# Keys made earlier in the step, list rows a step later, and a step's indirect DMAs in one row behind its scores

## The chip, the cores and the metric

The kernel runs on one core of a Trainium2 chip. Its five engines run side by side and meet on semaphores: TensorE (PE) multiplies matrices into the PSUM banks, VectorE (DVE) and ScalarE (ACT) work elementwise, GpSimd (POOL) does small arithmetic and issues the indirect DMAs, and SyncE (SP) issues the plain ones. The metric is the time of one execution on the device in microseconds (us), as a median of several runs.

## The reference

Input x is 128 sequences of 64 tokens with 128 features (8192 tokens), the context is as large, the mask is all ones. Two gated layers follow each other:

```
x = x + tanh(g_xattn[0]) * attention0(layernorm(x), ctx, ctx)     # q,k,v with biases; 16 heads of 8, softmax / sqrt(8)
x = x + tanh(g_ffn[0])   * experts0(layernorm(x))                 # 8 experts, top 2 by the router, gelu, 128->512->128
x = x + tanh(g_xattn[1]) * attention1(ctx, ctx, layernorm(x))     # per-head 8x8 weights, softmax / sqrt(128)
x = x + tanh(g_ffn[1])   * experts1(layernorm(x))                 # 4 experts, relu, gated by a depth per token
```

All of it is computed in float32; only the router's choice and the softmax's shift are split into parts of lower precision so that the sums stay exact.

## The kernel before, in words

**Steps.** The tokens of a layer's attention are cut into 32 groups of 256 tokens (two tiles of 128; `GROUPS`). Each engine runs a function `step(g)` once per group, written out in a fixed order; group g's scores stand in step g and what follows from them in the next steps: the values are multiplied by the probabilities in step g+1, heads and output projection come in step g+2, the second layer norm and the router in step g+3. A call `now(work, d)` does a piece of work for group g+d.

**A step of layer 0 on TensorE** turns the first quarter of the last group's probabilities (`probs_turned`, L1656), multiplies this group's keys and queries (`scores`, L1613: 32 small matmuls, keys stationary), turns the heads of group g-2 (L1588), turns the tokens of g+1 (L1632), projects the heads of g-2 (`project_out`, L1639), turns the rest of the probabilities, subtracts the maxima for two of the four score banks (`less_maximum`, L1623), and then multiplies probabilities by values for g-1 (`values_by_probs`, L1671, 32 small matmuls) and makes keys and queries of g+1 (`keys_queries`, L1687 and L1692) into the first bank of `ps_s`.

**On ScalarE** the step copies out what TensorE turned (PT, OT, xnT, xn2T), takes the exponentials (L813) and at its end copies the queries (qT, L777) and the keys in block-diagonal form (Kbd, L823, four operations). The next step's scores need those. `kept` is the copy of the summed values.

**VectorE** takes maxima (L1080), subtracts them, does the residual, the layer norms and, in every fourth step, the router's choice for a block of four groups; `route_places` (L1181 on) turns that choice into places in the lists.

**The lists.** Each token's row goes to the lists of its two experts in DRAM by an indirect DMA of 128 rows (`scatter`, L632), two per tile, 128 in all. `rows_due(k)` says which rows are issued in step k: the four of group k-8 from step 8 on, and near the end what the table `LAST_ROWS` says, up to six in a step. `scatter_at` spreads them over POOL's step at the points A to F, between waits for DVE's maxima, for the values product and for `xc`. When all of layer 0 is through, the rest of the rows follows, SyncE fills the lists' unused ends with zeros and loads the experts' tiles. In layer 1 the rows come back by indirect loads (`gather`, L675), four per step, likewise spread over the step.

**Banks.** `jobs` and `bank_free` say who used a bank of PSUM last and what TensorE must wait for before it writes the bank again.

Of the kernel before, what the change touches and what calls it, by code (L numbers as in the profile page):

```python
# [74 lines left out]
def at(u, k, mult=1, add=0, per=2):  # L75

    if isinstance(u, int):
# [11 lines left out]
LAST_ROWS = {24: ((16, 0, 1), (17, 0)), 25: ((17, 1), (18, 0, 1)), 26: ((19, 0, 1), (20, 0)), 27: ((20, 1), (21, 0, 1)),  # L89
             28: ((22, 0, 1), (23, 0)), 29: ((23, 1),), 30: ((24, 0, 1), (25, 0)), 31: ((25, 1),),  # L90
# [77 lines left out]
def build(nc, A, out):  # L168
    with ExitStack() as ctx:
# [169 lines left out]
        def late_to(n, batch, head):  # L339
# [15 lines left out]
        kq_bank, lg_bank, rk_bank = (ps_s[:, i, :] for i in range(3))  # L355
# [51 lines left out]
            "XT": (xnT_ready, 1, 1),  # L407
            "XT2": (xn2T_ready, 1, 1), "V": (v_ready, 1, 1)}

        def jobs(bank, g):  # L410

            if bank == 6:
                found = [("OT", g.plus(-2)), ("OUT", g.plus(-2))]
            else:
# [175 lines left out]
        def _(pool):  # L590
# [44 lines left out]
            def rows_due(k):  # L635

                due = LAST_ROWS.get(k, ((k - 8, 0, 1),) if 8 <= k < GROUPS else ())
                return [(n, slot, t) for n, *slots in due for slot in slots for t in range(2)]

            def scatter_at(g, point):  # L640

                rows = rows_due(g.k)
                spots = {2: "AD", 4: "ABCD", 6: "ABCDEF"}.get(len(rows), "")
                if point in spots:
                    scatter(*rows[spots.index(point)])
# [33 lines left out]
            def step(g):  # L679
# [13 lines left out]
                if have(0):  # L693
                    pool.wait_ge(max_done, g.count(4, 1))
                if g.layer == 0:
                    scatter_at(g, "A")
                elif have(4):
                    gather(g.plus(4), 0, 0)
                if g.layer == 1 and g.k in (GROUPS - 2, GROUPS - 1):
                    split_chunk(0, g.k - (GROUPS - 2))  # L700
                if have(0):
                    pool.wait_ge(max_done, g.count(4, 3))
                if g.layer == 0:
                    scatter_at(g, "B")
# [3 lines left out]
                elif have(4):  # L708
                    gather(g.plus(4), 0, 1)
# [1286 lines left out]
```

## Time and profile before

| | before |
|---|---|
| median of 3 runs | 1203.03 us (1202.12 to 1204.2) |
| the profiled execution's own time | 1202.05 us |
| its span in the trace | 1200.3 us |
| mean clock granted to TensorE, as a share of full speed | 0.963 |
| busy: PE / DVE / ACT / POOL | 1083.8 / 894.5 / 794.5 / 543.2 us |
| layer 0, first scores to last scores | 14.00 to 345.79 us |
| rest of layer 0, end of the lists | 345.79 to 404.44 us |
| layer 1, first scores to last scores | 678.46 to 966.06 us |

The profiled execution is one run, within the spread of the runs. Between 404 and 678 us stand the expert tiles of layer 0, after 970 us the dense experts of layer 1; the change doesn't touch either. A step is the time from the first matmul of one group's scores to that of the next. A duration in a row is that of the instruction or of a run of like instructions that abut; what stands in brackets is the idle time of the engine just before and what ended it, which is inferred from semaphore events ("remote" or "issue" stand where no instruction of this core is found to have ended just then).

### The profile page before, as it was taken

The page shows a single profiled execution, that of the slowest core. Times are in us where ns is not written, and L with a number is a line of the kernel's source. Part 1 is how long each engine was busy: PE and PEld are TensorE (multiplying, and loading weights), DVE is VectorE, ACT ScalarE, POOL GpSimd, SP SyncE. Part 2 cuts the span into 40 slices and gives each one's busy share as a digit, 9 for nine tenths or more (in the row PEclk, how much of TensorE's full clock was granted, in tenths as well). Part 3 has the DMA queues.
Part 4 walks back from the last instruction along what each step waited for, and adds up shares of the span by engine and source line. Part 5 has one row for each costly group of instructions (what it writes and reads, how often), then busy time and mean ns, then how long its engine had stood idle before and what let it go on. Part 6 is the DMA issues. An engine that isn't in the chain of part 4 may idle for free.

```text
span 1200.3 us, 38909 instructions
## 1 busy us (share of the span) xinstructions
PE 1083.8 (90%) x13205; PEld 918.0 (76%) x13205; DVE 894.5 (75%) x3003; ACT 794.5 (66%) x1739; POOL 543.2 (45%) x699
## 2 busy tenths in 40 slices
PE   7799999997885499999999699999999988999998
PEld 4677777775763499999999567666666767999997
DVE  5678887886777445545545779899898878988886
ACT  4788888886671255555555489999998964444443
POOL 2114555556547344344343676676666431222230
PEclk7999999999897699999999899999999999999999
DMA  7223211111101233333332211111221100000000
GB/s 195 86 86 94 78 55 54 53 51 56 49 22 55 82 98 102 96 93 96 93 95 77 57 50 49 50 48 47 51 50 46 32 2 10 27 17 17 26 17 27
DMA packets 116776, 71.81 MB, mean 60 GB/s; under 512 B 51736, under 2 KB 105240, under 8 KB 116632
## 3 DMA queue, kind: packets, MB, share of 16 engines
q1 hardware_dynamic: 108440, 53.13, 16.2%
q0 software_dynamic: 8192, 16.79, 4.5%
q8 instruction: 87, 1.43, 0.5%
q14 instruction: 57, 0.47, 0.1%
HBM read 45.88 MB, written 22.94 MB: 57 GB/s over the span
## 4 chain that ended last, share of the span: by engine, by line
PE 69%; DVE 10%; ACT 7%; issue 7%; SPq 4%; another core or an unknown queue 1%; POOL 1%; DMA 1%; DVEq 0%; ACTq 0%; POOLq 0%
PE ps_m L1902 11%; PE ps_p L1656 6%; PE ps_p L1781 5%; PE ps_m L1781 4%; PE ps_s L1613 4%; PE ps_p L1671 4%; PE ps_s L1888 3%; PE ps_s L1889 3%; PE ps_s L1890 3%; PE ps_s L1623 3%; PE ps_m L1639 3%; PE ps_s L1769 2%; PE ps_s L1771 2%; PE ps_s L1770 2%; PE ps_m L1588 2%
## 5 line engine op out<-in xcount | busy, mean ns | idle before, releaser
L776 ACT ACTIVATE PT<-ps_p 128x512 f32<-128x512 f32 x320 | 184.4, 596 | 32.3 <-PE ps_p L1656 18.2
L1080 DVE TENSOR_REDUCE mx<-ps_s 128x8 f32<-128x512 f32 x256 | 169.3, 683 | 36.8 <-PE ps_s L1613 23.4
L877 ACT ACTIVATE Kbd<-ps_s,c 128x512 f32<-128x512 f32 x128 | 87.4, 687 | 113.9 <-PE ps_s L1771 113.6
L592 POOL TENSOR_TENSOR spare<-spare 1x1 f32<-1x1 f32 x99 | 21.4, 216 | 295.0 <-DVE b1s L1459 152.1
L675 POOL DMA_INDIRECT w1a<-louts,gi x128 | 125.2, 978 | 54.9 <-issue 31.2
L1656 PE MATMUL ps_p<-cst,Pr 128*128 128x128 f32 x1024 | 148.6, 279 | 0.6 <-DVE orow L1376 0.4
L1902 PE MATMUL ps_m<-xn3T 128*128 128x128 f32 x1136 | 137.9, 275 | 0.0
L1902 PEld LDWEIGHTS ps_m<-xn3T 128*128 128x128 f32 x1136 | 132.7, 192 | 0.0
L958 ACT ACTIVATE xn3T<-ps_s,b1s 128x256 f32<-128x256 f32 x284 | 111.7, 474 | 28.3 <-PE ps_s L1890 28.3
L1656 PEld LDWEIGHTS ps_p<-cst,Pr 128*128 128x128 f32 x1024 | 121.6, 145 | 2.4 <-issue 1.7
L632 POOL DMA_INDIRECT lists<-xn3T,pos x80 | 78.4, 980 | 81.1 <-DVE mx L1080 54.2
L1566 DVE SCALAR_TENSOR_TENSOR x<-c,we,x 128x128 f32 x256 | 99.6, 451 | 11.5 <-DVE x L1572 6.4
L1480 DVE TENSOR_TENSOR xn3T<-ps_m,xn3T 128x256 f32<-128x256 f32 x71 | 30.1, 424 | 100.5 <-PE ps_m L1902 66.3
L776 ACT ACTIVATE rounded<-ps_p 128x256 fp32r<-128x256 f32 x71 | 27.3, 385 | 107.7 <-PE ps_p L1876 107.7
L1671 PE MATMUL ps_p<-PT,Vbd 128*18 128x64 f32 x4096 | 82.6, 221 | 10.8 <-issue 10.2
L1671 PEld LDWEIGHTS ps_p<-PT,Vbd 128*18 128x18 f32 x4096 | 65.2, 98 | 33.7 <-issue 27.9
L734 POOL TENSOR_TENSOR rounded<-w1a,rounded 128x512 fp32r<-128x512 f32 x71 | 89.6, 1261 | 0.0
L1888 PE MATMUL ps_s<-rounded 128*128 128x256 f32 x284 | 87.5, 308 | 0.0
L1613 PE MATMUL ps_s<-Kbd,qT 32*64 32x256 f32 x2048 | 74.8, 398 | 13.0 <-ACT Kbd L823 7.9
L1086 DVE TENSOR_TENSOR Pr<-ps_s,mx 128x512 f32<-128x512 f32 x128 | 84.1, 679 | 0.0
L601 POOL TENSOR_TENSOR ve<-mv,eps 128x4 f32<-128x4 f32 x72 | 15.5, 215 | 146.2 <-DVE mv L1022 136.7
L1889 PE MATMUL ps_s<-rounded 128*128 128x256 f32 x284 | 81.1, 285 | 0.0
(229 smaller groups left out, 2818.8 us busy)
## 6 DMA issues: line engine op xcount, KB each, us to landing
xn3T<-lists SPq DMA_DIRECT2D x71, 128.0 KB, 2.1
louts<-xn3T SPq DMA_DIRECT2D x71, 128.0 KB, 1.8
ctxg<-in_ctxT SPq DMA_DIRECT2D x32, 256.0 KB
Kbd<-in_ctxT SPq DMA_DIRECT2D x512, 8.0 KB
out<-x SPq DMA_DIRECT2D x16, 256.0 KB, 2.3
w1a<-in_L_ffn_W SPq DMA_DIRECT2D x8, 256.0 KB
w2a<-in_L_ffn_W SPq DMA_DIRECT2D x8, 256.0 KB
Pr<-in_ctxT SPq DMA_DIRECT2D x16, 128.0 KB, 2.3
```

What stands on the lines that cost most here:

```text
L675: nc.gpsimd.indirect_dma_start(ysb[g.par][:, s_, t, :], None, louts, bass.IndirectOffsetOnAxis(ap=gi[g.par][:, c:c + 1], axis=0)).then_inc ...
L776: return nc.scalar.activation(dst, src, ACT.Copy)
L958: nc.scalar.activation(hT[i][:, f, :], ps_s[:, 2 * i + f // 2, ET * (f % 2):ET * (f % 2 + 1)], ACT.Gelu_apprx_tanh, bias=b1s[k % 4][:, f:f ...
L1080: V.tensor_reduce(mx[g.par][:, q, :], per_key(ps_s[:, q, :]), AX, ALU.max).then_inc(max_done, 1)
L1566: V.scalar_tensor_tensor(tile, c2[:, e, :], flat(we[:, sl(u * 4 + t), e:e + 1]), tile, ALU.mult, ALU.add).then_inc(acc_b, 1)
L1613: ins = mm(ps_s[S * (b % 2):S * (b % 2) + S, q, GT * (b // 2):GT * (b // 2) + GT], qT[g.par][rows, S * b:S * b + S], Kbd[g.par][rows, b, : ...
L1656: ins = turn(ps_p[:, c % 2, P * i:P * i + P], Pr[g.par][:, j // 2, col:col + P], ident)
L1671: ins = mm(sums_bank[32 * i:32 * i + VW, col:col + S], Vbd[g.par][:, 2 * pr + b, j, :], PT[c][:, P * i + S * b:P * i + S * b + S], start=T ...
L1781: ins = mm(y_banks[k % 4][:, P * t:P * t + P], hD[k % 2][:, f, P * t:P * t + P], v2[:, c:c + P], start=(f == 0), stop=(f == FB1 - 1))
L1888: mm(o, w1h[i][:, w], xinTh[i], start=True, stop=False, skip_group_check=True)
L1889: mm(o, w1h[i][:, w], xinTl[i], start=False, stop=False, skip_group_check=True)
L1902: ins = mm(ps_m[:, i, P * t:P * t + P], hT[i][:, f, P * t:P * t + P], w2s[i][:, P * f:P * f + P], start=(f == 0), stop=(f == FB0 - 1))
```

## The change

1. **Keys early.** Layer 0's keys and queries are multiplied into bank 6 of PSUM instead of the first bank of `ps_s`. They wait for that bank's last reader, the residual of g-2 (`bank_free(..., "KQ")`), and no longer for the subtraction of this group. TensorE makes them ahead of `values_by_probs`, and `project_out` moves ahead of `tokens_turned`. ScalarE takes qT and the first two Kbd behind xn2T, then `kept`, the other two Kbd, and then the exponentials of banks 0 and 1; heads_out stands ahead of values. VectorE does the residual before the maximum of bank 0.
2. **Lists a step later.** `LAG = 9`; the table of the last rows is laid anew: six rows in steps 25 to 30 instead of 24 to 28 and 30.
3. **Indirect DMAs in a row.** A step's first four rows stand directly behind the wait for this group's scores; in a step of six the other two stand behind `inverse_deviations` and ahead of `rows_plus_constant`. In layer 1 three gathers stand behind the scores and the fourth behind `inverse_deviations`. The waits for `max_done`, `pv_done` and `on_ready` go.
4. **Last steps.** In steps 32 and 33 the first 3 and 5 rows come ahead of `inverse_deviations`.
5. **route_places** of the main blocks moves on VectorE from the step's start to behind `router_logits`.
6. The warming matmuls behind layer 0 also wait for one of the last scatters.

```diff
-LAST_ROWS = {24: ((16, 0, 1), (17, 0)), 25: ((17, 1), (18, 0, 1)), 26: ((19, 0, 1), (20, 0)), 27: ((20, 1), (21, 0, 1)),
-             28: ((22, 0, 1), (23, 0)), 29: ((23, 1),), 30: ((24, 0, 1), (25, 0)), 31: ((25, 1),),
+LAG = 9
+LAST_ROWS = {25: ((16, 0, 1), (17, 0)), 26: ((17, 1), (18, 0, 1)), 27: ((19, 0, 1), (20, 0)), 28: ((20, 1), (21, 0, 1)),
+             29: ((22, 0, 1), (23, 0)), 30: ((23, 1), (24, 0, 1)), 31: ((25, 0, 1),),
@@ gpsimd: step(g)
+                    early = {GROUPS: 3, GROUPS + 1: 5}.get(g.k, 0)
+                    for row in rows_due(g.k)[:early]:
+                        scatter(*row)
                     if have(-2):
                         inverse_deviations(g)
-                    if g.k == GROUPS:
-                        pool.wait_ge(pv_done, g.plus(-1).count(4, 4))
-                    for row in rows_due(g.k):
+                    for row in rows_due(g.k)[early:]:
                         scatter(*row)
                     return
                 if have(0):
-                    pool.wait_ge(max_done, g.count(4, 1))
+                    pool.wait_ge(s_done, g.count(4, 4))
                 if g.layer == 0:
-                    scatter_at(g, "A")
+                    for row in rows_due(g.k)[:4]:
+                        scatter(*row)
                 elif have(4):
                     gather(g.plus(4), 0, 0)
+                    gather(g.plus(4), 0, 1)
+                    gather(g.plus(4), 1, 0)
-                if have(0):
-                    pool.wait_ge(max_done, g.count(4, 3))
-                if g.layer == 0:
-                    scatter_at(g, "B")
-                    if have(-1) and rows_due(g.k):
-                        pool.wait_ge(pv_done, g.plus(-1).count(4, 4))
-                    scatter_at(g, "C")
                 if have(-2) or have(2):
                     inverse_deviations(g)
+                if g.layer == 0:
+                    for row in rows_due(g.k)[4:]:
+                        scatter(*row)
+                elif have(4):
+                    gather(g.plus(4), 1, 1)
                 if have(-1) and not (g.layer == 0 and g.k > LATE_SUMS):
                     rows_plus_constant(g.plus(-1))
-                if g.layer == 0:
-                    scatter_at(g, "D")
-                    if len(rows_due(g.k)) == 6:
-                        pool.wait_ge(on_ready, g.plus(-1).count(1, 1))
-                    scatter_at(g, "E")
-                    scatter_at(g, "F")
@@ scalar: step(g), layer 0
+                    now(heads_out, -2)
                     now(values, 0)
-                    now(heads_out, -2)
...
+                    now(queries, 1)
+                    now(keys, 1, (0, 1))
+                    now(sums_out, -1)
+                    now(keys, 1, (2, 3))
                     now(exps, 0, 0)
-                    now(sums_out, -1)
                     now(exps, 0, 1)
-                    now(keys_queries, 1)
@@ vector: step(g), layer 0
+                    now(residual, -2)
                     now(maximum, 0, 0)
-                    now(residual, -2)
...
+                    if placed and placed.in_main():
+                        route_places(placed, True)
                     now(denominators, -1)
@@ tensor: keys_queries(g) and step(g), layer 0
-                wait(pe, sub_done, g.count(2, -1))
                 if g.layer == 0:
+                    bank_free(pe, 6, g.plus(-1), "KQ")
                     pe.wait_ge(ctx_in[g.par], g.half_count())
-                    mm(kq_bank[:, 0:GT], wk[0][:, :], ctxg[g.par][:, :, 0, :], start=True, stop=True)
+                    mm(bank6[:, 0:GT], wk[0][:, :], ctxg[g.par][:, :, 0, :], start=True, stop=True)
...
+                    if g.k < GROUPS:
+                        now(project_out, -2)
                     now(tokens_turned, 1)
...
+                    now(keys_queries, 1)
                     now(values_by_probs, -1)
-                    now(keys_queries, 1)
```

ScalarE in one step of layer 0 from the values' copy to the last keys, before (PT, OT, xnT and xn2T are copies of turned tiles, Pr the exponentials, the PT between two Pr the copy `kept`):

```order
L776 ACTIVATE Vbd<-ps_m 64x32x8 x2
L776 ACTIVATE OT<-ps_m 128x256
L776 ACTIVATE PT<-ps_p 128x512
L776 ACTIVATE xnT<-ps_m 128x256
L776 ACTIVATE PT<-ps_p 128x512 x2
L813 ACTIVATE Pr<-ps_s 128x512 x2
L776 ACTIVATE xn2T<-ps_m 128x256
L813 ACTIVATE Pr<-Pr 128x512
L776 ACTIVATE PT<-ps_p 128x512
L813 ACTIVATE Pr<-Pr 128x512
L777 ACTIVATE qT<-ps_s,bcol 128x256
L823 ACTIVATE Kbd<-ps_s,bkm,cst 128x4x64 x4
```

and now:

```order
L763 ACTIVATE OT<-ps_m 128x256
L763 ACTIVATE Vbd<-ps_m 64x32x8 x2
L763 ACTIVATE PT<-ps_p 128x512
L763 ACTIVATE xnT<-ps_m 128x256
L763 ACTIVATE PT<-ps_p 128x512 x2
L800 ACTIVATE Pr<-ps_s 128x512 x2
L763 ACTIVATE xn2T<-ps_m 128x256
L764 ACTIVATE qT<-ps_m,bcol 128x256
L814 ACTIVATE Kbd<-ps_m,bkm,cst 128x4x64 x2
L763 ACTIVATE PT<-ps_p 128x512
L814 ACTIVATE Kbd<-ps_m,bkm,cst 128x4x64 x2
L800 ACTIVATE Pr<-Pr 128x512 x2
```

The exponentials of banks 0 and 1 moved from ahead of the queries and keys to behind them, and the heads ahead of the values.

POOL from one layer norm of a layer-0 step to the next, before, with the semaphores each waits for:

```order
L601 TENSOR_TENSOR ve<-mv,eps 128x4 [waits lnq_mv,lnf_mv]
L603 TENSOR_TENSOR rs<-ve,mhalf 128x4 [waits ln_ve]
L617 TENSOR_TENSOR xc<-x,orow 128x256 [waits x1_ready]
L632 DMA lists<-xn3T,pos 67584x128 [waits xn2_ready,pos_ready]
L632 DMA lists<-xn3T,pos 67584x128 [waits xn2_ready,pos_ready,max_done] x2
L632 DMA lists<-xn3T,pos 67584x128 [waits xn2_ready,pos_ready,pv_done]
```

and now:

```order
L605 TENSOR_TENSOR ve<-mv,eps 128x4 [waits lnq_mv,lnf_mv]
L607 TENSOR_TENSOR rs<-ve,mhalf 128x4 [waits ln_ve]
L621 TENSOR_TENSOR xc<-x,orow 128x256 [waits x1_ready]
L636 DMA lists<-xn3T,pos 67584x128 [waits xn2_ready,pos_ready,s_done]
L636 DMA lists<-xn3T,pos 67584x128 [waits xn2_ready,pos_ready] x3
```

The four DMAs, which were spaced by DVE's maxima and the values product, now stand in a row behind the scores (`s_done`), and none stands behind `xc`.

## Rows read from the trace of the kernel before

**Rows 1.** By stretch: us; PE, PEld, DVE, ACT, POOL busy (x); clock, DMA share, GB/s.

```profile
67.97:77.60 9.63, 9.07 (x150) 7.52 (x151) 7.31 (x25) 8.45 (x20) 1.92 (x3) 1.00 0.25 80
167.96:178.91 10.95, 10.01 (x159) 8.06 (x160) 10.54 (x43) 9.02 (x20) 6.45 (x8) 1.00 0.22 65
198.56:208.39 9.83, 9.34 (x150) 7.63 (x151) 7.40 (x25) 8.82 (x20) 5.88 (x8) 1.00 0.18 56
...
269.62:335.99 66.37, 52.02 (x766) 42.97 (x766) 46.81 (x185) 43.83 (x97) 36.52 (x42) 0.92 0.16 50
...
335.99:345.79 9.80, 9.33 (x150) 7.63 (x151) 7.67 (x27) 8.52 (x20) 4.99 (x6) 1.00 0.07 23
...
735.75:745.08 9.33, 8.41 (x148) 6.22 (x144) 8.38 (x29) 8.42 (x20) 5.49 (x8) 1.00 0.19 48
745.08:754.16 9.08, 8.50 (x148) 6.28 (x144) 8.28 (x29) 8.68 (x21) 6.76 (x10) 1.00 0.20 50
```

**Rows 2.** Chain that ended last, 176 to 207 us: start, length, what.

```profile
188.79 1.12 PE ps_s L1613 x32
...
196.48 1.83 ACT Kbd L823 x4
...
198.56 1.12 PE ps_s L1613 x32
...
202.17 0.87 PE ps_s L1623 x4
```

**Rows 3.** Timeline of ScalarE in the step before 198.56 us: start, length, instruction.

```profile
192.98 1.09 ACT L813 ACTIVATE Pr<-ps_s 128x512 f32<-128x512 f32 x2
...
195.44 0.62 ACT L813 ACTIVATE Pr<-Pr 128x512 f32<-128x512 f32 x1
```

**Rows 4.** Timeline, 268 to 276 us, all engines.

```profile
268.72 0.60 PE L1656 MATMUL ps_p<-cst,Pr 128*128 128x128 f32 x4
...
269.45 1.03 POOL L632 DMA_INDIRECT lists<-xn3T,pos  x1 [0.18 <-issue]
...
269.62 1.12 PE L1613 MATMUL ps_s<-Kbd,qT 32*64 32x256 f32 x32 [0.29 <-ACT Kbd L823]
...
270.78 0.96 POOL L632 DMA_INDIRECT lists<-xn3T,pos  x1 [0.30 <-issue]
...
272.05 0.96 POOL L632 DMA_INDIRECT lists<-xn3T,pos  x1 [0.30 <-issue]
273.62 1.29 DVE L1080 TENSOR_REDUCE mx<-ps_s 128x8 f32<-128x512 f32 x2 [2.29 <-remote]
273.79 0.38 ACT L776 ACTIVATE OT<-ps_m 128x256 f32<-128x256 f32 x1 [3.17 <-remote]
```

**Rows 5.** Waits, 260 to 350 us: total, times, longest.

```profile
ACT OT L776 <- remote: 17.7, 6, 3.2
```

**Rows 6.** Timeline, 362 to 370 us.

```profile
365.39 0.41 PE L1588 MATMUL ps_m<-cst,On 128*128 128x128 f32 x2 [1.00 <-DVE On L1114]
...
365.83 0.96 POOL L632 DMA_INDIRECT lists<-xn3T,pos_end  x1 [0.30 <-issue]
365.84 0.38 ACT L776 ACTIVATE OT<-ps_m 128x256 f32<-128x256 f32 x1 [2.28 <-issue]
...
366.98 0.41 PE L1731 MATMUL ps_s<-wr,xn2T 128*64 128x8 f32 x8
...
368.84 0.17 DVE L1121 COPY lgb<-ps_s 128x16 f32<-128x16 f32 x1 [0.52 <-PE ps_s L1731]
```

**Rows 7.** Timeline, 735 to 745 us, layer 1.

```profile
736.43 0.97 POOL L675 DMA_INDIRECT w1a<-louts,gi  x1 [0.16 <-issue]
...
737.87 1.29 DVE L1080 TENSOR_REDUCE mx<-ps_s 128x8 f32<-128x512 f32 x2 [0.65 <-PE ps_s L1613]
```

**Rows 8.** Timeline, 376 to 406 us: the last scatter, then the tile load.

```profile
394.40 0.96 POOL L632 DMA_INDIRECT lists<-xn3T,pos_end  x1 [0.30 <-issue]
...
403.24 2.74 SPq L540 DMA_DIRECT2D xn3T<-lists  x3
```

More of the change, by code:

```diff
@@ L353, in build @@
         kept = PT[0]
-        kq_bank, lg_bank, rk_bank = (ps_s[:, i, :] for i in range(3))
+        kq_banks = (bank6, ps_s[:, 0, :])
+        lg_bank, rk_bank = ps_s[:, 1, :], ps_s[:, 2, :]
         ones_ready, arrays_in = sem("ones_ready"), sem("arrays_in")
@@ L635, in rows_due @@
             def rows_due(k):
-                due = LAST_ROWS.get(k, ((k - 8, 0, 1),) if 8 <= k < GROUPS else ())
+                due = LAST_ROWS.get(k, ((k - LAG, 0, 1),) if LAG <= k < GROUPS else ())
                 return [(n, slot, t) for n, *slots in due for slot in slots for t in range(2)]
[L640 to L645, printed above, removed]
             def split(src, high, low, out_sem, number, spot=0):
@@ L820, in keys_queries, with keys @@
                 if g.layer == 0:
-                    copy(qT[g.par][:, :], kq_bank[:, GT:2 * GT], bcol[:, 0:1])
-                    for i in range(4):
-                        ins = nc.scalar.activation(Kbd[g.par][:, :, i, :], kq_bank[:, 0:GT].rearrange("p (b k) -> p b k", b=4),
-                                                   ACT.Identity, bias=bkm[:, i:i + 1], scale=blk[:, i:i + 1])
+                    copy(qT[g.par][:, :], bank6[:, GT:2 * GT], bcol[:, 0:1])
+                else:
+                    copy(qT[g.par][:, :], kq_banks[1][:, GT:2 * GT]).then_inc(kq_ready, 1)
+            def keys(g, some):
+                for i in some:
+                    ins = nc.scalar.activation(Kbd[g.par][:, :, i, :], bank6[:, 0:GT].rearrange("p (b k) -> p b k", b=4),
+                                               ACT.Identity, bias=bkm[:, i:i + 1], scale=blk[:, i:i + 1])
+                if 3 in some:
                     ins.then_inc(kq_ready, 1)
-                else:
-                    copy(qT[g.par][:, :], kq_bank[:, GT:2 * GT]).then_inc(kq_ready, 1)
             def values(g):
@@ L924, in step @@
                     now(sums_out, -1)
-                    now(keys_queries, 1)
+                    now(queries, 1)
                     now(exps, 0, 0)
@@ L1264, in step @@
                         layer1_constants()
-                    block = router_due(g, -5, 1)
-                    if block:
-                        route_places(block, block.k not in AT_ONCE)
+                    placed = router_due(g, -5, 1)
+                    if placed and not placed.in_main():
+                        route_places(placed, placed.k not in AT_ONCE)
                     now(maximum, 0, 2)
@@ L1690, in keys_queries @@
                     pe.wait_ge(v1_odd, GROUPS // 2)
+                else:
+                    pe.wait_ge(sub_done, g.count(2, -1))
                 pe.wait_ge(xnT_ready, g.count(1, 1))
-                mm(kq_bank[:, GT:2 * GT], wq[g.layer][:, :], xnT[g.par][:, :], start=True, stop=True).then_inc(kq_done, 1)
+                mm(kq_banks[g.layer][:, GT:2 * GT], wq[g.layer][:, :], xnT[g.par][:, :], start=True, stop=True).then_inc(kq_done, 1)
             def values(g):
@@ L1803, in step @@
                         ranks(Group(0, GROUPS - 2, 0), g)
-                    now(project_out, -2)
+                    if g.k >= GROUPS:
+                        now(project_out, -2)
                     if g.k == GROUPS:
@@ L1812, in step @@
                         now(tokens2_turned, -3)
+                    now(keys_queries, 1)
                     now(values_by_probs, -1)
-                    now(keys_queries, 1)
                     if g.k != GROUPS:
```

14 lines of the change are left out of this document (6 added, 8 removed).

## The prediction

> **What bounds the kernel now.** I read three views: the busy time by stretch, the chain of waits inside one step, and timelines around each indirect DMA. A plain step of layer 0 with its four scatters takes 9.83 us, and TensorE is busy for 9.34 of it, ScalarE for 8.82, VectorE for 7.40; a step without scatters takes 9.63 with TensorE at 9.07 [rows 1]. So TensorE is nearly full, and what is left is a loop: ScalarE's four Kbd end at 196.48 + 1.83 = 198.31, the next scores start at 198.56 [rows 2], 0.25 later. Every fourth step holds the router's choice for a block: 10.95 us, VectorE busy for 10.54 of it [rows 1]; VectorE bounds that one.
>
> The tail is another matter. Five steps from 269.62 to 335.99 take 66.37 us, 13.3 each, with TensorE busy for 52.0 at a granted clock of 0.92, while the next takes 9.80 [rows 1]. The timeline shows why. Three scatters are issued at 269.45, 270.78 and 272.05; the scores stand at 269.62 and end at 270.74, but VectorE's maximum, which waits for them alone, starts at 273.62 after 2.29 us of idleness, and ScalarE's copy of the heads at 273.79 after 3.17, both 0.6 to 0.8 us behind the end of the last scatter at 273.01 [rows 4]. That happens six times, 17.7 us in all before the heads' copy [rows 5]. I read it as a hold: a result of TensorE's that comes due while an indirect DMA is being issued is announced only when it, and any that follows at once, is over. These are the steps that issue six rows, whose last three reach into the next scores. In layer 1 it is milder: a gather at 736.43 lies over the end of the scores, the maximum starts at 737.87 after 0.65 of idleness, and that step takes 9.33 against 9.08 for its neighbour [rows 1, 7].
>
> Is every result held? At 365.39 TensorE turns the heads in the middle of a row of scatters; ScalarE copies them at 365.84, at once, though a scatter starts at 365.83. But in the same row router logits that start at 366.98 are read only at 368.84 [rows 6]. So some kinds of result pass and others don't: I take the scores, the values product and the router logits (all of many small matmuls) as held and turns and projections as free.
>
> **The change part by part.**
>
> *Keys early, layer 0.* The exponentials of banks 0 and 1 (0.62 us each [rows 3]) go behind the keys. ScalarE's work is the same, so it ends when it did, at 198.31; now the exponential of bank 0 ends one exponential earlier, at 197.7. The probabilities' first turn (0.60 for four, [rows 4], of which some 0.45 before what follows can start) comes on TensorE ahead of the scores, so the scores could start at about 198.2 instead of 198.56: 0.3 to 0.4 gained. The residual before the maximum of bank 0 costs nothing on VectorE, which has over 2 us of slack in a plain step [rows 1]. The keys' bank must wait for the residual of g-2; that is done behind project_out, which now stands earlier, so I put this wait at nothing; it costs up to 0.4 us a step if the residual is late (the VectorE maxima ahead of it are 0.65 each [rows 4]).
>
> *The row of four.* Scores end 1.12 behind the step's start, the row starts at about 1.5, and at the tail's spacing of 1.27 (272.05 - 270.78 [rows 4]) its last ends near 6.3. Then nothing is issued until the next scores, so they are never held. The values product, which TensorE starts in this step at about 4.7 (the last less_maximum ends at 203.04 - 198.56 = 4.5 [rows 2]), now behind the keys, comes due at 6.5 or later, as the row ends. Of the 0.27 us that TensorE is busier with scatters than without [rows 1] I take back a part: 0.1. Together a plain step goes from 9.83 to 9.40; the floor is TensorE's 9.07, the other end no gain.
> Steps 4 to 6 have no scatters: 3 x 0.36 = 1.1. Twelve plain steps from 9 to 24: 12 x 0.43 = 5.2 (0 to 9). The block steps stay with VectorE: five together 0.5, for route_places moved.
>
> *The tail.* Seven steps, 24 to 30: 9.8 + 66.4 + 9.8 = 86.0 now. Six of them will have six rows: four behind the scores and two behind inverse_deviations, which waits for VectorE's statistics and so comes in the last third of the step. The second can still lie over the next scores' end by the gather's pattern, at a price of about 0.95 (one scatter, 0.96 [rows 4], not three). A plain one is then 9.4 + 0.95 = 10.35, a block one 10.95 and about half of that price, 11.4. So 9.4 + 3 x 10.35 + 3 x 11.4 = 74.7. Gain 11.3. Its ends: 0 if all three still lie there, and 17.4 if none is held (7 x 9.8 = 68.6). That the lists come a step later adds none: POOL issues 128 scatters in either.
>
> *Behind the last scores* (345.79 to 404.44, 58.7 us [rows 1]). The held scores of step 31 cost one of the six long waits; its price falls from some 2 us to 1: 1.0. The last scatter is issued at 394.40 and the first tile is read at 403.24 [rows 8]. With 3 and 5 rows ahead of the deviations POOL's idleness there shrinks; against it the tail carries over as many rows. I take 1.5 (0 to 4.5).
>
> *The warming matmuls* wait longer, in a stretch in which TensorE is idle anyway: nothing.
>
> *Layer 1.* The fourth gather goes from behind xc (over the scores' end) to right behind the deviations, and the three others into a row: the 0.25 between 9.33 and 9.08 [rows 1] goes in every second of about 30 steps: 3.5. Against it the row may hold other results: bounds 4 either way.
>
> Sum: 1.1 + 5.2 + 0.5 + 11.3 + 1.0 + 1.5 + 3.5 = 24.1. On the profiled execution's 1202.05 that is 1177.9; the median of the runs lies 1.0 above it, so the forecast is 1179, with 1172 to 1189 as its own range.
>
> A rule of the Trainium skill speaks against the largest term. The page "SBUF — State Buffer", section "Who interferes with whom", says that "PE and ACT never wait on anyone" and that a DMA doesn't contend with a compute engine. By it the scatters could not be what delays the maximum at 273.62, and laying them anew would bring the tail nothing: that would be the second rival below, its sum. The rows don't contradict its words (it speaks of memory ports, not of when a result is announced), but they show the waits ending behind the last scatter; I go by the rows.
>
> **Rivals.**
>
> *A, slower: less_maximum is held by the row.* It comes due at 4.5 in the step, in the middle of a row that runs from 1.5 to 6.3; held until 0.5 behind that it comes at 6.8. The exponentials of banks 2 and 3 started at 192.98, 4.2 behind the scores at 188.79 [rows 2, 3]; they would start 2.6 later, and since qT and the keys now stand behind them, the loop takes that over but for the 0.4 gained and the 0.3 to 0.4 in which ScalarE idles or waits today: a plain step takes 9.83 + 2.6 - 0.8 = 11.6. Steps 9 to 24: 12 x 1.75 + 4 x 0.8 = 24.2 lost; steps 25 to 31 lose what the tail gains (7 x 1.75 = 12.3 against 11.3); -1.1, -2.5 and -3.5 as above: +18, so 1221. It decides from the point at which less_maximum counts with the scores rather than with the turns. For it: the logits in [rows 6], due in a row and held. Against it: the heads' turn there, which was not. If the turns of heads were held too it would be far worse, at 5 us a step. Chance 0.18.
>
> *B, C: the gain is in one place only.* B: the steady steps stay (VectorE or the keys' bank wait sets them), the tail gains 8.5 and the rest as above: 1202.05 - 8.5 - 2.5 - 3.5 + 1 = 1188.5; TensorE's 9.34 of 9.83 speaks for it. Chance 0.15. C: the two rows behind the deviations still meet the scores, and with them the whole hold: the tail gains nothing, the rest stays, 12.8: 1202.05 - 12.8 + 1 = 1190. Chance 0.11.
>
> *D: it does nothing.* The hold is of something else than the row's place, and the clock and the loop give back the rest: 1201 to 1205. Chance 0.06.
>
> **How the numbers follow.** The forecast, 1179, has 0.50. The range must leave out no more than 0.2: it ends at 1168 (the tail without any hold and plain steps near the floor) and at 1209, which leaves out most of A. About 0.2% (2.4 us) is what a measurement of this kernel can tell from no change. Faster: the forecast, B and C, 0.76; slower: A and a part of D, 0.20; the same 0.04.
>
> **What would show it.** Right: plain steps at 9.4 with scores directly behind the exponential of bank 0 and its turn; tail steps of 10 to 12 with the "remote" waits of the heads' copy gone or under 1.5; TensorE's clock at 1.0 there; layer-1 steps even at 9.1. Wrong: exponentials of banks 2 and 3 that start at 6 to 7 behind the scores, each behind the end of the row (A); VectorE's idle time ended by the project_out or ScalarE's by VectorE with steps of 9.8 (B); long waits of the maximum behind the scatters that follow inverse_deviations (C).

## The result, and the profile after

The changed kernel takes 1229.21 us (median of 4 runs, 1225.09 to 1231.19) where the kernel before takes 1202.57: ratio 1.0205 with a 95% interval of 1.017 to 1.024. It is slower by 27 us; 1179 was forecast. One more thing has to be said at once, since no later number can be read without it: on three of the six chips used for the experiments the kernel before takes 1203 to 1204 us, as here, and on three it takes 1153 to 1154. The changed kernel is slower on both kinds: by 27 us here, its only timing on the first kind, and by 0.9% (1.0052 to 1.0122) on the second.

Busy time of the changed kernel by stretch: layer 0's steps, the rest of layer 0, layer 1's steps, the rest; then a step without scatters, a plain step with four, steps 25 to 30, and a step of layer 1. Columns as in [rows 1].

```profile
14.62:350.62 336.00, 295.20 (x4591) 235.58 (x4591) 262.26 (x901) 267.66 (x579) 155.93 (x189) 0.98 0.23 68
350.62:679.96 329.34, 297.10 (x2584) 281.61 (x2584) 181.07 (x645) 167.74 (x422) 145.36 (x193) 0.94 0.31 85
679.96:996.67 316.71, 268.38 (x4346) 193.95 (x4343) 247.25 (x839) 252.66 (x571) 182.73 (x242) 0.97 0.18 42
996.67:1226.90 230.23, 219.74 (x1670) 198.87 (x1666) 196.65 (x590) 103.28 (x164) 50.19 (x67) 0.99 0.07 19
77.92:87.09 9.17, 9.04 (x151) 7.41 (x151) 7.41 (x25) 8.58 (x21) 1.94 (x4) 1.00 0.29 88
194.18:204.60 10.42, 9.65 (x150) 7.69 (x151) 7.47 (x26) 8.68 (x20) 5.86 (x7) 1.00 0.18 52
...
280.74:350.62 69.88, 60.69 (x916) 48.20 (x916) 56.02 (x211) 52.44 (x115) 45.30 (x51) 0.98 0.18 54
806.76:817.31 10.55, 8.77 (x148) 6.32 (x144) 8.15 (x29) 8.34 (x21) 6.03 (x8) 1.00 0.19 43
```

Before, the same four stretches took 331.8, 332.7, 287.6 and 234.2 us. So layer 0's steps lose 4.2, the rest of layer 0 gains 3.3, layer 1's steps lose 29.1, the end gains 4.0 and the start loses 0.6: 26.6 in all, the difference of the spans. Two of these are partly chance. Layer 0's second step, before any scatter, takes 11 to 16.5 us from one kernel's trace to the next (16.49 here, 13.37 before, 13.41 in e1, which has the same layer 0), and that is 3.1 of the 4.2. The end takes 231 to 234 us in the traces of set 1 below, whatever the kernel, so its 4.0 is no gain of the change. The loss is layer 1's, where the change does nothing but move gathers. TensorE's work there has hardly grown (268.4 for 263.5 us); it waits.

What it waits for is shown by ScalarE's timeline in that step of layer 1, with TensorE's turns and the gathers beside it (changed kernel, start, length, instruction):

```profile
808.08 0.60 PE L1650 MATMUL ps_p<-cst,Pr 128*128 128x128 f32 x4
...
808.30 0.99 POOL L672 DMA_INDIRECT w1a<-louts,gi  x1 [2.37 <-PE ps_s L1607]
...
808.72 0.60 ACT L763 ACTIVATE PT<-ps_p 128x512 f32<-128x512 f32 x1
...
809.33 1.04 PE L1650 MATMUL ps_p<-cst,Pr 128*128 128x128 f32 x8
...
809.60 0.95 POOL L672 DMA_INDIRECT w1a<-louts,gi  x1 [0.31 <-issue]
...
810.25 0.59 ACT L763 ACTIVATE PT<-ps_p 128x512 f32<-128x512 f32 x1
...
810.85 0.95 POOL L672 DMA_INDIRECT w1a<-louts,gi  x1 [0.30 <-issue]
...
812.71 0.60 ACT L763 ACTIVATE PT<-ps_p 128x512 f32<-128x512 f32 x1 [1.87 <-remote]
```

TensorE's last turn of the probabilities ends at 810.37. ScalarE has been free since 810.84 and copies it only at 812.71, 0.9 behind the end of the last gather. It is the picture of [rows 4], now in most steps and at the turn instead of the scores: in 25 of the 31 steps of layer 1 this copy waits for 1.0 to 1.9 us. ScalarE then has everything behind this copy late: Vbd, the exponentials, qT. Not every result is late beside a gather: the turn that ends at 808.68, 0.38 us into the first gather, is copied at 808.72.

Layer 0 has the same, smaller (changed kernel, ScalarE and POOL in the step from 194.18):

```profile
197.06 0.96 POOL L636 DMA_INDIRECT lists<-xn3T,pos  x1 [0.30 <-issue]
198.33 0.96 POOL L636 DMA_INDIRECT lists<-xn3T,pos  x1 [0.30 <-issue]
199.59 0.96 POOL L636 DMA_INDIRECT lists<-xn3T,pos  x1 [0.31 <-issue]
...
199.29 0.60 ACT L763 ACTIVATE PT<-ps_p 128x512 f32<-128x512 f32 x1 [0.96 <-PE ps_p L1650]
...
201.56 0.47 ACT L764 ACTIVATE qT<-ps_m,bcol 128x256 f32<-128x256 f32 x1 [0.42 <-PE ps_m L1688]
```

0.96 us are lost at the last turn and 0.42 at the queries' product (made in one piece of work with the keys'), 1.38 in all; the step takes 10.42, 1.25 more than the 9.17 of a step without scatters. In most other plain steps the shares are different: 0.2 to 0.3 at the last turn, 0.1 at each of the next two copies and 0.4 to 0.9 at the queries' product.

### The profile page after: what moved, and what is told of

Its sections match the earlier page's. It is cut to its first block, busy times and chain, and to the rows that moved or that the text cites. A ratio compares the mean times of both kernels' runs of the same rounds, so it can differ in the third digit from the quotient of the medians.

```text
span 1226.9 us, 38871 instructions
## 1 busy us (share of the span) xinstructions
PE 1088.8 (89%) x13205; PEld 914.5 (75%) x13205; DVE 892.4 (73%) x3003; ACT 795.4 (65%) x1739; POOL 540.4 (44%) x699
## 4 chain that ended last, share of the span: by engine, by line
PE 66%; issue 12%; ACT 7%; DVE 6%; SPq 3%; another core or an unknown queue 3%; POOL 1%; DMA 1%; DVEq 0%; ACTq 0%; POOLq 0%
PE ps_m L1903 10%; PE ps_p L1650 6%; PE ps_s L1607 4%; PE ps_p L1778 4%; PE ps_m L1778 4%; PE ps_p L1665 4%; PE ps_s L1889 3%; PE ps_s L1890 3%; PE ps_s L1891 3%; PE ps_p L1673 3%; PE ps_s L1768 2%; PE ps_s L1766 2%; PE ps_s L1617 2%; PE ps_s L1767 2%
## 5 line engine op out<-in xcount | busy, mean ns | idle before, releaser
L763 ACT ACTIVATE PT<-ps_p 128x512 f32<-128x512 f32 x320 | 190.2, 599 | 71.5 <-remote 35.5
L1072 DVE TENSOR_REDUCE mx<-ps_s 128x8 f32<-128x512 f32 x256 | 166.7, 682 | 13.8 <-PE ps_s L1607 13.0
L1665 PE MATMUL ps_p<-PT,Vbd 128*18 128x64 f32 x4096 | 92.2, 223 | 29.1 <-issue 27.9
L1665 PEld LDWEIGHTS ps_p<-PT,Vbd 128*18 128x18 f32 x4096 | 68.7, 99 | 62.9 <-issue 57.7
L605 POOL TENSOR_TENSOR ve<-mv,eps 128x4 f32<-128x4 f32 x72 | 14.9, 208 | 173.5 <-DVE mv L1014 161.6
L1889 PE MATMUL ps_s<-rounded 128*128 128x256 f32 x284 | 87.4, 308 | 0.0
L800 ACT ACTIVATE Pr<-ps_s 128x512 f32<-128x512 f32 x128 | 71.1, 596 | 16.2 <-PE ps_s L1617 5.7
L1100 DVE RECIPROCAL rden<-ps_p 128x32 f32<-128x32 f32 x64 | 22.8, 356 | 80.3 <-PE ps_p L1673 74.4
```

The source lines that it names most:

```text
L763: return nc.scalar.activation(dst, src, ACT.Copy)
L1072: V.tensor_reduce(mx[g.par][:, q, :], per_key(ps_s[:, q, :]), AX, ALU.max).then_inc(max_done, 1)
L1665: ins = mm(sums_bank[32 * i:32 * i + VW, col:col + S], Vbd[g.par][:, 2 * pr + b, j, :], PT[c][:, P * i + S * b:P * i + S * b + S], start=T ...
L1889: mm(o, w1h[i][:, w], xinTh[i], start=True, stop=False, skip_group_check=True)
```

## The experiments

Theory 1: the issue of an indirect DMA holds back the announcement of TensorE's results, of the turns too, and a row of them behind the scores meets the results that ScalarE waits for. (That the trace gives a result as finished doesn't tell whether the result or only its announcement is late, since the profile models the ends of matmuls; no run here separates the two.) Its rivals stand in the expectations. The kernels were run in sets, each set on one chip beside the kernel before.

| set | kernel before | kernel | median | ratio, 95% interval |
|---|---|---|---|---|
| 1 | 1203.5 | gathers spaced (e1) | 1196.2 | 0.9942 (0.9925 to 0.9958) |
| 1 | | all spaced (e2) | 1201.6 | 0.9993 (0.9971 to 1.0015) |
| 1 | | before, gathers in a row (e3) | 1219.9 | 1.0143 (1.0103 to 1.0183) |
| 1 | | two and two (e4) | 1213.3 | 1.0085 (1.0064 to 1.0105) |
| 2 | 1153.2 | GpSimd work for gathers (e5) | 1150.9 | 0.9980 (0.9963 to 0.9997) |
| 2 | | narrow gathers (e6) | 1162.3 | 1.0073 (1.0050 to 1.0096) |
| 2 | | three and one (e7) | 1144.7 | 0.9936 (0.9917 to 0.9955) |
| 2 | | three and one, places first (e8) | 1145.6 | 0.9935 (0.9917 to 0.9954) |
| 3 | 1154.0 | changed kernel again (r1) | 1163.5 | 1.0087 (1.0052 to 1.0122) |
| 3 | | as e5 (r2) / as e7 (r3) | 1151.8 / 1147.8 | 0.9995 / 0.9954 |
| 4 | 1202.9 | fourth gather behind xc (f1) | 1217.0 | 1.0109 (1.0082 to 1.0136) |
| 4 | | as e5 (f2) | 1182.1 | 0.9824 (0.9801 to 0.9846) |
| 5 | 1153.1 | as e7 (g1) | 1147.3 | 0.9935 (0.9913 to 0.9957) |
| 5 | | as e6 (g2) | 1164.5 | 1.0096 (1.0069 to 1.0122) |
| 5 | | as f1 (g3) | 1148.9 | 0.9969 (0.9949 to 0.9988) |
| 6 | 1203.6 | as e7 (h1) | 1186.5 | 0.9871 (0.9848 to 0.9894) |

**Which part costs: gathers spaced (e1), and the row alone in the kernel before (e3).**

```diff
 # e1, layer 1, on the changed kernel
-                    gather(g.plus(4), 0, 0)
-                    gather(g.plus(4), 0, 1)
-                    gather(g.plus(4), 1, 0)     # behind s_done, in a row
-                    gather(g.plus(4), 1, 1)     # behind inverse_deviations, ahead of xc
+                    gather(g.plus(4), 0, 0)     # behind max_done 1
+                    gather(g.plus(4), 0, 1)     # behind max_done 3
+                    gather(g.plus(4), 1, 0)     # behind inverse_deviations
+                    gather(g.plus(4), 1, 1)     # behind xc
 # e3: the same lines the other way round, on the kernel before
```

> The changed kernel with layer 1's four gathers put back to their four places (layer 0 as changed). Theory 1 (the row of three gathers behind the scores holds TensorE's results that come due beside it: the last turn of the probabilities, less_maximum): layer 1's steps fall from 10.3 to about 9.2 us and the kernel from 1229 to about 1200. Rival 2 (layer 1 is slower for another part of the change, such as the keys' bank or the two kernels' other code): steps stay above 10 and the time stays above 1220.

> The kernel before with one part of the change alone: layer 1's gathers as three in a row behind the scores and the fourth behind inverse_deviations. Theory 1: layer 1's steps go from 9.2 to about 10.3 us, 1203 + 29 = 1232. Rival 2: within 3 us of 1203.

e1: 1196.2, and layer 1's steps take 287.5 us again, as before. e3: 1219.9, 16 above the kernel before, with steps of 9.9 to 10.1. Both say that the order of the gathers makes layer 1 slow and that the rest of the change doesn't do it by itself; rival 2 falls. But e3 lost 16 where 29 were expected. GpSimd's order in its layer 1 is that of the changed kernel, the fourth gather ahead of xc included, and its gathers start at the same places in the step; yet its stretch takes 305.3 us and not 316.7, and the copy of the last turn waits for 1.0 us and not 1.8:

```profile
678.75:984.07 305.32, 264.36 (x4346) 192.52 (x4343) 247.53 (x838) 254.02 (x571) 182.50 (x242) 0.98 0.18 44
```

The 11 us between them stay open. The changed kernel wasn't timed beside e3, so the chip may be the difference, or something else of the change that counts only together with the row.

**All spaced (e2).**

```diff
-                    for row in rows_due(g.k)[:4]:    # behind s_done
-                        scatter(*row)
+                    scatter_at(g, "A")               # and B to F, at their places in the kernel before
```

> The changed kernel with all indirect DMAs spaced as before in both layers: what is left is keys early, lists a step later, route_places moved. Theory 1: plain steps with scatters at 9.3 to 9.5 us, since keys early is worth the 0.5 us it shows in steps without scatters (9.17 for 9.65); the tail still has holds of 2 to 3 us; about 1192 (1186 to 1197). Rival 3 (the new order on ScalarE and TensorE costs by itself as soon as scatters are issued at all): steps at 10 or more, 1203 or more.

1201.6: no better than the kernel before. Theory 1 had 1192, a miss; rival 3's steps of 10 or more weren't there either. Of four steps three took 9.17, 9.88 and 9.87, and the block step 11.77 for 10.95. The keys' earlier place is used up by two things: a spaced scatter still meets the scores (waits of 0.77 us for the heads' turn, 0.42 without a scatter), and VectorE, as the block step below shows. In the tail, steps of up to 14.9 stayed.

**Two and two (e4).**

```diff
-                    for row in rows_due(g.k)[:4]:
+                    for row in rows_due(g.k)[:2]:    # the others behind inverse_deviations; gathers likewise
```

> The changed kernel with two of a step's indirect DMAs behind the scores and all others behind inverse_deviations, in both layers. Theory 1 (what counts is which results come due within 1.5 us behind an issue): the pair behind the scores ends before less_maximum, the pair behind the deviations begins as the values product is over, so plain steps take 9.4 and layer 1's 9.3, about 1190 (1183 to 1198); in the six-row steps four stand behind the deviations and run into the next scores, so these stay near 12 to 13. Rival 4 (any indirect DMA directly behind the scores costs, however many follow): 1210 or more.

1213.3, a miss by 23. inverse_deviations comes later in the step than I had put it, so the pair behind it falls on the next scores (this kernel, around scores at 146.89):

```profile
146.68 1.03 POOL L636 DMA_INDIRECT lists<-xn3T,pos  x1 [0.20 <-issue]
146.89 1.12 PE L1607 MATMUL ps_s<-Kbd,qT 32*64 32x256 f32 x32
148.02 0.96 POOL L636 DMA_INDIRECT lists<-xn3T,pos  x1 [0.30 <-issue]
149.50 1.29 DVE L1072 TENSOR_REDUCE mx<-ps_s 128x8 f32<-128x512 f32 x2 [1.61 <-remote]
```

The scores end at 148.01 and are read at 149.50, 0.5 behind the end of the second scatter. Two of the six-row steps took 20.5 and 20.7 us. The time is in rival 4's range, but its reason doesn't hold: plain steps in which only the pair behind the scores is issued beside them take 9.2, and layer 1's take 9.5. Theory 1 survives, but its timing of where the second pair falls didn't, and no run put that right.

**The mechanism itself (e5, f2): GpSimd work in the place of the three gathers.**

```diff
-                    gather(g.plus(4), 0, 0)          # and 0, 1 and 1, 0
+                    stand_in(g.plus(4), 0, 0)        # tensor_tensor(..., eps4, mhalf, ALU.pow), 128x4
...
-                dve.wait_ge(gathered[g.par], g.u * (32 * STEPS) + 64 * (g.k // 2 + 1))
+                dve.wait_ge(gathered[g.par], 64 * (g.k // 2 + 1) if g.k < 4 else 128 + 16 * (g.k // 2 - 1))
```

> The changed kernel in which the three gathers of layer 1's row are left out for groups 4 to 31 and a small power operation on GpSimd of about the same length (1.04 us for 128x4) stands in each one's place; layer 1's sums of the experts are therefore made from old rows. Theory 1 (the issue of an indirect DMA is what holds TensorE's results): layer 1's steps fall from 10.3 to 9.1 or less, the kernel from 1229 to about 1197. Rival 5 (GpSimd being busy directly behind the scores, or what it reads, is enough): steps stay at 10.0 or more, 1222 or more.

> As r2_no_dma_again: layer 1's row of three gathers replaced by GpSimd operations of their length. On a chip with the hold, theory 1: layer 1's steps 8.6 to 9.1 instead of 10.3; rival 5 (GpSimd being busy is enough): 10.0 or more. On a chip without: 1151 as twice before.

Set 2 (and 3) turned out to be of the kind of chip where the kernel before takes 1153, and couldn't decide this. In set 4 the kernel before took 1202.9, and f2 1182.1 (2 runs): layer 1's steps take 8.6 and 9.0 us in turn, as in set 2, and GpSimd is as busy as ever (busy 188.5 us of the stretch, 182.7 in the changed kernel):

```profile
675.39:948.28 272.89, 259.87 (x4346) 186.81 (x4342) 260.09 (x838) 248.52 (x571) 188.54 (x242) 0.98 0.13 29
```

On the same chip f1 (the changed kernel but for the fourth gather's place, below), with the three gathers in their row, takes 307.9 us for this stretch, and f2 272.9, while its layer 0 still has the slow 10.3 us steps beside its scatters. e5, in set 2, takes 272.9 as well: without the row the two kinds of chip are equal in layer 1. So the indirect DMAs make the results late, and GpSimd's being busy doesn't; rival 5 falls. This is the run that shows it. Its 35 us are more than the lateness alone, since leaving the gathers out saves 8 to 9 us on chips without it too (282.1 in r1; 272.9 in e5 and 274.0 in r2). VectorE's wait for the gathered rows had to be lowered with them; in the changed kernel VectorE never stood idle for it in the step shown, so that isn't what was saved.

**Narrow gathers (e6, g2).** The three gathers fetch rows of 16 numbers.

> The changed kernel in which the three gathers of layer 1's row fetch 16 numbers per row instead of 128 (the same 128 descriptors each, an eighth of the bytes; layer 1 then uses wrong rows). Theory 1a (what holds is the making of the descriptors on GpSimd): steps stay at 10.3, 1226 to 1231. Rival 1b (what holds is the transfer of the rows into SBUF): steps fall to 9.3 or less, about 1200.

Both runs fell on chips without the hold, so whether descriptors or bytes hold stays open. They gave 9.15 us a step, as the full gathers do there.

**Two kinds of chip (r0, r1).** The kernel before and the changed kernel again.

> The kernel before once more, for its trace beside the others of this set. The same kernel took 1203.5 us in the first set of experiments and 1153.2 in the second, on another chip. Theory 9 (the chips differ in whether an indirect DMA holds TensorE's results): where it takes about 1153, the waits of VectorE's maximum and ScalarE's copy behind TensorE's finished results (2.3 and 3.2 us in the trace of 1202 us) are gone and tail steps are near 10 us; where it takes about 1203 they are there.

> The changed kernel once more. Theory 9: on a chip where the kernel before takes 1153 it is not slower by 2% but within 1% of it: layer 0 gains as predicted (plain steps 9.17, tail steps near 10 to 11), layer 1 stays at about 9.15 against 8.6 to 9.0. On a chip where the kernel before takes 1203 it takes 1225 to 1231 again.

The profiled run of the kernel before took 1156.5 there. Its tail, at the same place as [rows 4], scatters of a six-row step over the scores:

```profile
270.28 1.03 POOL L632 DMA_INDIRECT lists<-xn3T,pos  x1 [0.18 <-issue]
...
270.45 1.12 PE L1613 MATMUL ps_s<-Kbd,qT 32*64 32x256 f32 x32 [0.55 <-ACT Kbd L823]
...
271.62 0.96 POOL L632 DMA_INDIRECT lists<-xn3T,pos  x1 [0.30 <-issue]
...
271.85 0.68 DVE L1080 TENSOR_REDUCE mx<-ps_s 128x8 f32<-128x512 f32 x1
```

The scores end at 271.57 and are read at 271.85, while a scatter is being issued. The scatters take as long as on the other chips (0.98 us) and TensorE's granted clock is nearly the same (0.97 for 0.96); the hold is missing. Layer 0's plain steps take 9.62 instead of 9.83, layer 1's 8.57 instead of 9.2, the tail steps 9.6 to 10.6 instead of 12.2 to 14.2.

TensorE's results aren't all that is late on the other kind of chip. SyncE's eight copies of zeros into the lists' ends are issued while scatters run; this is the kernel before, first in the trace of 1202 us and then on this chip:

```profile
379.75 21.36 SPq L529 DMA_DIRECT2D lists<-zero  x8
```

```profile
362.47 8.15 SPq L529 DMA_DIRECT2D lists<-zero  x8
```

The slow ones end at 401.11, behind the last scatter (once the scatters are over, they too start 1.1 us apart, as all eight do on this chip), and the first tile of the lists is loaded 8.8 us behind that scatter [rows 8] instead of 3.0. This splits the traces as the times do: 7.4 to 9.5 us in all nine traces on chips with the hold, 3.0 in all eleven on chips without. So some 6 of the 50 us between the kinds have nothing to do with TensorE's results, and what the two delays have in common is the scatter beside them.

Layer 1's steps in the kernel before and in the changed one, on this chip:

```profile
652.85:921.54 268.69, 255.84 (x4346) 187.92 (x4342) 248.16 (x836) 248.66 (x571) 186.33 (x242) 0.97 0.21 50
```

```profile
645.63:927.72 282.09, 263.81 (x4347) 188.18 (x4343) 266.48 (x835) 249.94 (x571) 183.74 (x242) 0.97 0.20 47
```

The change still costs 13.4 us there, and this time VectorE's busy time has grown, by 18.3. Theory 9 holds, with a second loss that it didn't explain.

**The second loss (f1, g3): the fourth gather behind xc.**

```diff
-                elif have(4):
-                    gather(g.plus(4), 1, 1)
                 if have(-1) and not (g.layer == 0 and g.k > LATE_SUMS):
                     rows_plus_constant(g.plus(-1))
+                if g.layer == 1 and have(4):
+                    gather(g.plus(4), 1, 1)
```

The groups on VectorE that grew, first in the kernel before and then in the changed one, on the chip of set 3:

```profile
L1061 DVE SCALAR_TENSOR_TENSOR nb<-mv,rs 128x4 f32<-128x4 f32 x23 | 6.9, 300 | 0.1
L1220 DVE SCALAR_TENSOR_TENSOR t<-t,dw 128x128 f32<-128x128 f32 x23 | 6.4, 279 | 0.0
```

```profile
L1212 DVE SCALAR_TENSOR_TENSOR t<-t,dw 128x128 f32<-128x128 f32 x22 | 19.0, 866 | 0.0
L1053 DVE SCALAR_TENSOR_TENSOR nb<-mv,rs 128x4 f32<-128x4 f32 x22 | 13.9, 631 | 0.0
```

and what runs beside them in the changed kernel:

```profile
793.18 0.65 DVE L1053 SCALAR_TENSOR_TENSOR nb<-mv,rs 128x4 f32<-128x4 f32 x1
793.75 0.93 DVE L1212 SCALAR_TENSOR_TENSOR t<-t,dw 128x128 f32<-128x128 f32 x1
793.78 0.74 POOL L621 TENSOR_TENSOR xc<-x,orow 128x256 f32<-128x256 f32 x1
```

> The changed kernel with one instruction moved: layer 1's fourth gather stands behind xc (rows_plus_constant) again, the three others stay in their row behind the scores. Theory 10 (where results aren't held, the changed kernel's layer 1 takes 9.14 a step instead of 8.57 because xc, moved behind the fourth gather, runs beside VectorE's L1053 and L1212 and slows them from 0.30 to 0.63 and from 0.28 to 0.87 us): there layer 1's steps fall to 8.6 to 8.7 and the kernel from 1163.5 to about 1149. Rival 11 (the row of three itself takes the time): 9.1 as before, 1163. On a chip with the hold no theory gives it more than 5 us, since VectorE doesn't bound there.

> As f1_fourth_behind_xc. On a chip without the hold, theory 10 (xc beside VectorE's L1053 and L1212): layer 1's steps 8.6 to 8.7, about 1149; rival 11 (the row of three itself): 9.1, 1163. On a chip with the hold: 1217 again.

g3 gave 1148.9, the 1149 expected: layer 1's steps are 8.56, and L1212 takes 0.284 us on average again. So on these chips the fourth gather's place was the whole second loss, and the row of three costs nothing. That it acts through xc is shown for L1212 alone. L1053 starts 0.60 ahead of xc, beside the fourth gather (issued from 792.73 to 793.75), and ends 0.08 behind that. And in the kernel before xc starts with the same VectorE operation, but there it is xc that gets longer, 0.85 for 0.74 us (r0):

```profile
792.90 0.28 DVE L1220 SCALAR_TENSOR_TENSOR t<-t,dw 128x128 f32<-128x128 f32 x1
792.91 0.85 POOL L617 TENSOR_TENSOR xc<-x,orow 128x256 f32<-128x256 f32 x1
```

Which of the two pays, no run here decides. The Trainium skill's page "SBUF — State Buffer", section "Who interferes with whom", says that a VectorE instruction with two inputs in SBUF contends with a GpSimd instruction that reads SBUF; the rows agree, 0.28 becoming 0.87 us beside xc. On a chip with the hold f1 took 12 us less than the changed kernel on its own chip, which no theory had (at most 5 was expected): steps of 9.9 to 10.1 for 10.1 to 10.5. There the last turn is read 5.1 us behind the scores' start instead of 5.9, with the row of three at the same place. But e3 reads it at 5.1 too and has steps of 9.9 to 10.1, with the fourth gather still ahead of xc. So the 12 us can't be put down to the moved gather; like e3's 11 they stay open.

**A row that escapes (e7, r3, g1, h1).** Gathers spaced; in layer 0 three scatters behind the scores, the fourth behind the values product.

```diff
-                    for row in rows_due(g.k)[:4]:
+                    for row in rows_due(g.k)[:3]:
                         scatter(*row)
...
+                if g.layer == 0 and have(-1) and rows_due(g.k):
+                    pool.wait_ge(pv_done, g.plus(-1).count(4, 4))
+                if g.layer == 0:
+                    for row in rows_due(g.k)[3:4]:
+                        scatter(*row)
                 if have(-2) or have(2):
                     inverse_deviations(g)
```

> Layer 1's gathers spaced as before; in layer 0 three scatters in a row behind the scores and the fourth behind the values product of g-1, ahead of inverse_deviations (any further ones behind it). Theory 1 (of the row of four only the last hurts, as it meets the keys' product and the values product): plain steps of layer 0 fall from 10.4 to 9.2 to 9.5, block steps to 11.3 to 11.7, and the kernel from 1196 (with the row of four) to about 1183. Rival 6 (the first three do the harm): steps stay at 10.3, 1196.

> As e7_three_and_one. On a chip with the hold, theory 1: plain steps of layer 0 fall from 10.4 to 9.2 to 9.5 and the time to 1183 or so (before 1203); rival 6 (the first three scatters do the harm): 10.3, 1196. On a chip without: 1145 to 1148 again.

It beats both kernels on both kinds of chip: 1144.7, 1147.8 and 1147.3 where the kernel before takes 1153 to 1154, and 1186.5 where it takes 1203.6 (0.9871, 0.9848 to 0.9894). Against e1, which differs only in layer 0's scatters but ran on another chip of the same kind, its stretch of layer 0 (h1) falls from 332.1 to 319.7 us, of which 2.3 stand in the second step, which differs by chance; the medians, each against the kernel before of its set, differ by 9.7:

```profile
14.15:333.87 319.72, 290.54 (x4591) 231.86 (x4591) 260.94 (x901) 264.45 (x579) 153.91 (x188) 0.98 0.24 71
```

So the fourth scatter, on the keys' and values products, did more than half of the harm to layer 0's plain steps (10.4 to 9.7 on average, where 9.2 is without scatters), and rival 6 falls. Not all: plain steps are 9.4 to 10.2 where 9.2 to 9.5 were expected, and a copy or exponential still waits (ScalarE, 0.77 us for less_maximum):

```profile
191.90 0.60 ACT L811 ACTIVATE Pr<-ps_s 128x512 f32<-128x512 f32 x1 [0.77 <-PE ps_s L1628]
```

**route_places (e8).** The main blocks' call is back at the start of VectorE's step.

> The kernel of e7_three_and_one with route_places of the main blocks back at the start of VectorE's step. Theory 7 (route_places between router_logits and the denominators is what makes block steps of 11.3 without any scatter, 10.7 before): block steps fall by 0.5 to 0.7, some 8 of them, 4 to 6 us less than e7_three_and_one. Rival 8 (the exponentials of banks 0 and 1, now last on ScalarE, make VectorE's long step late): block steps and time unchanged within 2 us.

1145.6 for 1144.7, block steps 11.8 in both: theory 7 falls. Rival 8's number came true; its reason, the late exponentials, wasn't tried by itself. A block step and the step ahead of it, which holds first_choice, take 20.85 us in the kernel before (r0) and 20.96 in e7's kernel (r3):

```profile
159.70:180.55 20.85, 18.67 (x310) 15.30 (x310) 18.21 (x66) 17.28 (x39) 12.54 (x15) 1.00 0.20 64
```

```profile
155.23:176.19 20.96, 18.91 (x310) 15.10 (x310) 19.04 (x68) 18.34 (x41) 12.83 (x16) 1.00 0.21 66
```

The step ahead is shorter by 0.45 and the block step longer by 0.6: VectorE's work bounds the pair, and what the first gains the second gives back. That VectorE is the bound of the pair is read from the chain, not tried.

## Why the prediction was wrong

**What bounds the kernel.** The hold was read rightly where it stands: scatters over the scores. The step that failed is the sentence "I take the scores, the values product and the router logits (all of many small matmuls) as held and turns and projections as free". It rested on one row of scatters beside one turn [rows 6]. In the changed kernel the copy of the last turn of the probabilities waits for 1.0 to 1.9 us in 25 of the 31 steps of layer 1. In layer 0's plain steps it waits for 0.2 to 1.0, and that of the queries' product for 0.4 to 0.9. Other turns do pass (808.68, above), so it isn't the kind of matmul that decides; what does is open.

**Keys early.** Right in mechanism where nothing is issued: 9.17 for 9.65 in steps 4 to 6, 0.5 each for the 0.36 forecast. In block steps it is given back, 11.3 for 10.7 even without scatters; forecast was 0.5 gained in all five.

**The row of four.** Forecast 9.40, measured 10.42; steps 9 to 23 took 162.7 us for 152.1. That the values product "comes due at 6.5 or later, as the row ends" was not what mattered: the last turn and the queries' product come due inside it. That was rival A's mechanism in kind, with the turn ahead of less_maximum as the first result to be held, but smaller: the exponentials of banks 2 and 3 start 5.2 to 6.1 behind the scores and not at 6 to 7, and a plain step is 10.4 and not 11.6. A's forecast of 1221 for the kernel was only 8 off, by luck: it had 24 us lost in layer 0's steps and 3.5 gained in layer 1; layer 0's steps lost 4.2 and layer 1's 29.1.

**The tail.** Steps 24 to 30 take 80.3 for 86.0: 5.7 gained for 11.3 forecast. Each also carries what the row costs over its forecast, 1.0 us, which in six steps would be all that is missing (a sum; no run shows it by itself). The long holds over the scores did go, and TensorE's granted clock there is 0.98 for 0.92 [rows 1].

**Behind the last scores.** 3.3 gained for 2.5: right in size. 2.3 of it lie between the last scores and the last scatter; how much the held scores of step 31 had in it isn't shown.

**Layer 1.** Forecast 3.5 gained with bounds of 4 either way, measured 29.1 lost. This is the mis-sized term that decides. I took the row of three to remove one hold and priced what it adds as "may hold other results", within 4 us, with no row behind that bound. One held result a step, at anything from the 0.65 us of [rows 7] to the 2.3 of [rows 4], would have been 18 to 64 us over 28 steps. The row of three accounts for 18 to 20 of the 29 (e3's 305.3 and f1's 307.9 us against 287.6 and e1's 287.5), whether the fourth gather stands ahead of xc or behind it; what made the other 9 to 11 was not found.

**The rule** on the Trainium skill's page "SBUF — State Buffer", section "Who interferes with whom", that "PE and ACT never wait on anyone" would have made the hold nothing. f2 shows that taking the row of indirect DMAs away, with GpSimd as busy, takes 35 us out of layer 1 on the same chip; the measurement decides, though what waits may be the announcement and not a memory port.

## What to carry to other kernels

Before moving asynchronous issues into a row, list which results of the other engines come due while the row is issued and who waits for them; price each at a hold that the trace already shows, in every step, until a run shows otherwise. Three scatters behind the scores and one behind the values product were worth about 10 us over four in a row: place an issue where no result that an engine waits for comes due beside it. Time a small change of order on more than one chip, as what binds here is there or not by the chip.

## What the runs showed of the hardware that I had not expected

- Chips differ by 50 us (4%) on the same kernel: about 1203 on three of those used in the experiments and about 1153 on three, with nearly the same granted clock (0.96 and 0.97) and the same 0.98 us per scatter. On the first kind TensorE's results are read late beside indirect DMAs, and SyncE's eight copies of zeros beside the scatters take 16 to 22 us instead of 8 to 9. What makes a chip one or the other was not found.
- On chips that hold, the delay is not simply until the issue is over: the last turn was read 5.1 us behind the scores' start in e3 and f1 and 5.9 in the changed kernel, with the row of three at the same place in the step, while a turn that ended 0.38 us into the first gather was read at once.
- A GpSimd addition of 0.74 us can make a VectorE operation that starts with it take 0.87 to 0.93 instead of 0.28 (r1); in r0, started within 0.01 us of each other, the VectorE operation kept its 0.28 and the addition took 0.85.
